# The last slot of a mixture-of-experts stage is activated and rounded in pairs of column blocks, with its remainders and its sum on VectorE

## The chip, the cores and the metric

One core of a Trainium2 chip runs the whole program. The metric is the device time of one execution in microseconds (us); shown is the median of three. The engines are PE (TensorE: matmuls, with its weight loads as PEld), DVE (VectorE), ACT (ScalarE), POOL (GpSimd) and SP (SyncE, which here only issues transfers). A name with q behind it (ACTq, POOLq) is the sequencer of that engine.

## The reference

Three residual blocks on x of 64 x 32 tokens with 256 features; the change touches the last one.

```python
x = x + xattn(layernorm(x), ctx_768)          # 16 heads over 257 context rows
x = x + local_attention(layernorm(x))         # window of 5 tokens
# third block: 8 experts, each token goes to one
logits = t @ Wr + br;  e = argmax(logits)     # t = layernorm(x), 2048 tokens
h = gelu(t @ W1[e] + b1[e])                   # 256 -> 1024
h = gelu(h @ W2[e] + b2[e])                   # 1024 -> 512
x = x + h @ W3[e] + b3[e]                     # 512 -> 256
```

## The kernel before, in words

**Slots.** Once every token has its expert, the tokens are grouped by expert into slots of 128 rows; there are always SLOTS = (2048 + 8 * 127) // 128 = 23 of them, numbered 0 to 22. A slot's rows are fetched from a buffer in DRAM by an indirect transfer (`gather_slot`, L671), which brings the residual row and the normalised row, and the result is written to the output by another (`scatter_slot`, L701); both are issued by POOL. `bounds_check=N_TOKENS - 1` is the highest row that such a transfer may touch, given as a number. `slot_x` and `y` have AHEAD = 5 buffers. Slots 0 to 19 run partly in loops, and 20, 21 and 22 are written out with constant numbers.

**Precision.** Each matrix is kept as a rounded part (HI) and the remainder (LO), and a product is the sum of three: HI x HI, HI x LO, LO x HI (`PRODUCTS`, the activations' part first). So every activation is rounded by ACT into its HI tile, and POOL subtracts that from the exact value into the LO tile.

**One slot through the engines.** PE turns the 256 normalised features (`turn_x`, L1479), multiplies by W1 in two halves (`layer1`, L1488), and turns the result `z1` into eight blocks of 128 x 128, four to a half (`turn_z1`, L1520). ACT adds the bias and applies Gelu block by block (`first_layer`: four ACTIVATE at L853, then one rounding copy of the half at L857), POOL takes the remainder of each half (`lo_h1`, L686), and PE multiplies by W2 with 24 matmuls of 512 columns (`layer2`, L1536: 8 HI x HI, 8 HI x LO, 8 LO x HI). ACT copies the result to `z2` (`copy_z2`, L844), PE turns it (`turn_z2`, four transposes, L1544), ACT applies the second Gelu (`second_layer`: four ACTIVATE at L863, one rounding at L867), POOL takes the remainder (`lo_h2`, L690), and PE multiplies by W3 (`layer3`: one matmul for the bias row at L1551, then 12 of 256 columns at L1556, the last four with the LO part). The product lands in the one bank `ps_y`; ACT copies it to `y` (`copy_y`, L840), which also frees the bank for the next slot (`y_copied`), POOL adds the residual rows (`add_residual`, L696) and issues the scatter.

**Order around the end.** The order of every engine is written out by hand. For slots 21 and 22 it is:

- PE: layer2(21), turn_z1(22), turn_z2(21), layer2(22), layer3(21), turn_z2(22), layer3(22). The third layer of slot 21 is kept back (`postponed`) so that PE has work while ACT copies z2 of slot 22.
- ACT: copy_z2(21), first_layer(22), second_layer(21), copy_z2(22), copy_y(21), second_layer(22), copy_y(22).
- POOL: lo_h1(22), lo_h2(21), add_residual(21), scatter_slot(21), lo_h2(22), add_residual(22), scatter_slot(22).
- DVE splits the experts' weights into HI and LO (L1202, L1205) and has nothing after that.
- SP waits at L514 until all scatters have landed. Every engine then ends with a DRAIN (L52), the end of the block.

`keep_clock(n)` (L1276) issues n transposes of the identity into a bank that is not in use, and computes nothing. It stands before the change in the drain of the attention stages and, with n = 34, ahead of slot 0.

Of the kernel before, what the change touches and what calls it, by code (L numbers as in the profile page):

```python
# [12 lines left out]
ALU = mybir.AluOpType  # L13
AX = mybir.AxisListType

P = 128
# [4 lines left out]
def perceiver_kernel(nc, x, ctx_turned, last_turned, mask, Wq, Wk, Wv, Wo, lWq_turned, lbq, lWk_turned, lbk, lWv, lbv,  # L21
# [30 lines left out]
    with ExitStack() as stack:  # L52
# [10 lines left out]
        def sem(name):  # L63
            return stack.enter_context(nc.semaphore(name))
# [196 lines left out]
        y_filled = sem("y_filled")  # L261
        y_copied = sem("y_copied")
        y_done = sem("y_done")
        y_stored = [sem(f"y_stored{i}") for i in range(AHEAD)]
        w_in = sem("w_in")
        wq_in = sem("wq_in")
# [114 lines left out]
        def turned_rows(i):  # L381

            return (xT_parts_1, xT_raw_1) if isinstance(i, int) and i == 1 else (xT_parts, xT_raw)

        def last_but_one(i):
            return follows(i, 1) and not follows(i, 2)
# [130 lines left out]
        def _(pool):  # L517
# [145 lines left out]

            over_tiles(pool, iteration)

            def gather_slot(i):
                q = i % AHEAD
                if i >= AHEAD:
                    pool.wait_ge(y_done, i - AHEAD + 1)
                    pool.wait_ge(y_stored[q], 16 * (i // AHEAD))  # L670
                g.indirect_dma_start(out=slot_x[:, q, :], out_offset=None, in_=rows_dram,  # L671
                                     in_offset=bass.IndirectOffsetOnAxis(ap=slot_ids[:, i, 0:1], axis=0),
                                     bounds_check=N_TOKENS - 1, oob_is_err=False).then_inc(slot_in[q], 16)

            def lo_xT(i):
                pool.wait_ge(xT_hi_done, i + 1)
# [5 lines left out]
            def lo_h1(i):  # L682
                for half in range(2):
                    fs = slice(half * F1 // P // 2, (half + 1) * F1 // P // 2)
                    pool.wait_ge(h1_hi_done, 2 * i + half + 1)
                    g.tensor_tensor(h1_parts[LO][:, fs, :], h1[:, fs, :], h1_parts[HI][:, fs, :].bitcast(F32), ALU.subtract).then_inc(h1_done, 1)  # L686

            def lo_h2(i):
# [8 lines left out]

            def scatter_slot(i):
                q = i % AHEAD
                pool.wait_ge(y_done, i + 1)  # L700
                g.indirect_dma_start(out=out_rows, out_offset=bass.IndirectOffsetOnAxis(ap=slot_ids[:, i, 1:2], axis=0),  # L701
                                     in_=y[:, q, :], in_offset=None, bounds_check=N_TOKENS - 1, oob_is_err=False).then_inc(y_stored[q], 16)

            pool.wait_ge(rows_done, 16 * TILES)
            pool.wait_ge(route, MAPPED)
            gather_slot(0)
# [7 lines left out]
            for i in range(SLOTS):  # L714
                if i > 0:
                    add_residual(i - 1)
                if i + 3 < SLOTS:
                    gather_slot(i + 3)
                if i > 0:
                    scatter_slot(i - 1)  # L720
                if i + 2 < SLOTS:
                    lo_xT(i + 2)
                if not last_but_one(i):
                    lo_h2(i)
                if i + 1 < SLOTS:
                    lo_h1(i + 1)
                if last_but_one(i):
                    lo_h2(i)
            add_residual(SLOTS - 1)
            scatter_slot(SLOTS - 1)  # L730

        @block.scalar
        def _(act):
# [112 lines left out]
            def first_layer(i, e):  # L846

                for half in range(2):
# [7 lines left out]
                    act.wait_ge(gelu1_done, 2 * i + half + 1)  # L856
                    a.copy(h1_parts[HI][:, 4 * half:4 * half + 4, :], h1[:, 4 * half:4 * half + 4, :]).then_inc(h1_hi_done, 1)  # L857

            def second_layer(i, e):
                act.wait_ge(t2_filled, i + 1)  # L860
                alone(act)
                for c in range(F2 // P):
                    last = a.activation(h2[:, c, :], ps_t2[:, c * P:(c + 1) * P], ACT.Gelu,  # L863
                                        bias=bias_cols[:, bass.ds(e * (F2 // P) + E * F1 // P + c, 1)])
                last.then_inc(gelu2_done, 1)
                act.wait_ge(gelu2_done, i + 1)
                a.copy(h2_parts[HI], h2).then_inc(h2_hi_done, 1)  # L867
# [22 lines left out]

            def slot(i, run, q):
                copy_z2(i)
                if not follows(i, 1):
                    copy_y(i - 1, q - 1)
                if follows(i, 2):
                    copy_xT(i + 2)
                if not last_but_one(i):
                    second_layer(i, expert_of(i))
                if follows(i, 1):
                    first_layer(i + 1, expert_of(i + 1))  # L900
                if last_but_one(i):
                    second_layer(i, expert_of(i))
                if follows(i, 2):
                    copy_z1(i + 2)
                if not last_but_one(i):
                    copy_y(i, q)

            over_slots(act, slot)

# [1 line left out]
        def _(dve):  # L911
# [275 lines left out]
            for first_matrix, e in EARLY + LATE:  # L1187
                w, raw, buffers, w_in_buffer, ready = ((w1, w1_raw, BUFFERS1, w1_in, w1_ready) if first_matrix else
                                                      (w23, w23_raw, BUFFERS23, w23_in, w23_ready))
                b = e % buffers  # L1190
                pieces = [(w_in_buffer[b], slice(0, COLS1))] if first_matrix else zip(w_in_buffer[b], PIECES)
                for n, (piece_in, columns) in enumerate(pieces):
                    dve.wait_ge(piece_in, 16 * (e // buffers + 1))
                    if not first_matrix and e == 1 and n == 0:
                        dve.wait_ge(b3_split, 1)
                    early = (e, None if first_matrix else n) in ROUNDED_EARLY
                    if early:
                        dve.wait_ge(early_rounded, ROUNDED_EARLY.index((e, None if first_matrix else n)) + 1)
                    for at in range(columns.start, columns.stop, 512):
                        part = slice(at, at + 512)  # L1200
                        if not early:
                            d.tensor_copy(w[:, b, HI, part], raw[:, b, part]).then_inc(rounded, 1)  # L1202
                            k += 1
                            dve.wait_ge(rounded, k)
                        last = d.tensor_tensor(w[:, b, LO, part], raw[:, b, part], f32(w[:, b, HI, part]), ALU.subtract)  # L1205
                        if at + 512 == columns.stop:
                            last.then_inc(ready, 1)
                        elif early:
                            last.then_inc(rounded, 1)
                            k += 1  # L1210
                            dve.wait_ge(rounded, k)

        @block.tensor
        def _(pe):
# [312 lines left out]
            def layer2(i, e):  # L1527
                pe.wait_ge(z2_copied, i)
                for products in (PRODUCTS[0:2], PRODUCTS[2:3]):
                    for half in range(2):  # L1530
                        pe.wait_ge(w23_ready, 3 * e + half + 1)
                        for hp, wp in products:
                            for f in range(4 * half, 4 * half + 4):
                                if wp == HI and f == 4 * half:
                                    pe.wait_ge(h1_done if hp == LO else h1_hi_done, 2 * i + half + 1)
                                last = t.matmul(ps_z2[:, :], h1_parts[hp][:, f, :], weight(w23, e % BUFFERS23, wp, f * F2, F2),  # L1536
                                                start=(hp == HI and wp == HI and f == 0), stop=(hp == LO and f == F1 // P - 1))
                last.then_inc(z2_filled, 1)
# [5 lines left out]
                    last = t.transpose(ps_t2[:, c * P:(c + 1) * P], z2[:, c * P:(c + 1) * P], ident[:, :])  # L1544
                last.then_inc(t2_filled, 1)

            def layer3(i, e):
# [4 lines left out]
                for hp, wp in PRODUCTS:  # L1552
                    if hp == LO:
                        pe.wait_ge(h2_done, i + 1)
                    for c in range(F2 // P):
                        last = t.matmul(ps_y[:, 0:D], h2_parts[hp][:, c, :], weight(w23, e % BUFFERS23, wp, W3_AT + c * D, D),  # L1556
                                        start=False, stop=(hp == LO and c == F2 // P - 1))
                last.then_inc(y_filled, 1)

            def expert_of(i):  # L1560
# [11 lines left out]
            def slot(i, run, q):  # L1572
                expert = expert_of(i)
                layer2(i, expert)
                if postponed:
                    layer3(i - 1, postponed.pop())
                if follows(i, 2):
                    ahead = expert_of(i + 2)
                    turn_x(i + 2, run + (q + 2) // AHEAD, (q + 2) % AHEAD)
# [47 lines left out]
```

## Time and profile before

| what | value |
|---|---|
| median of 3 executions | 760.08 us |
| lowest, highest | 759.63, 761.08 us |
| the profiled execution, its own time | 763.91 us |
| span of the instructions in its trace | 762.2 us |
| mean granted TensorE clock in it | 0.972 of 2.4 GHz |
| busy: PE, PEld, DVE, ACT, POOL | 94%, 80%, 62%, 59%, 57% of the span |
| chain of work that ended last | PE 85%, DVE 7%, ACT 2%, POOL 1% of the span |

The profiled execution took 763.91 us, of which 762.2 us lie between its first and its last instruction; it is 3.83 us above the median of the unprofiled ones. Times inside the trace count from the first instruction. A granted clock of 1.00 is 2.4 GHz and 0.50 is 1.2 GHz.

### The profile page before, as it was taken

What the parts mean: (1) busy time and instruction counts of PE and PEld (TensorE: products, weight loads), DVE (VectorE), ACT (ScalarE), POOL (GpSimd) and SP (SyncE); (2) the same over time, 40 slices, a digit from 0 to 9 for tenths busy, and PEclk for the clock granted to TensorE, in tenths of its full rate; (3) what the DMA queues carried; (4) which work ended last, traced back from release to release, by engine and by line L of the source; (5) the groups of instructions that cost most, each with busy time, mean ns of one, the idle gap of its engine ahead of it and who ended that gap; (6) DMA issues with size and microseconds to landing.
All of it is one profiled execution on the core that took longest, in us unless ns stands there. A gap on an engine that the chain in (4) does not pass through costs nothing.

```text
span 762.2 us, 26478 instructions
## 1 busy us (share of the span) xinstructions
PE 717.5 (94%) x9229; PEld 609.4 (80%) x9230; DVE 472.0 (62%) x1377; ACT 452.8 (59%) x1072; POOL 431.3 (57%) x565
## 2 busy tenths in 40 slices
PE   8999999999999999999999648999999999997994
PEld 7788888888888888888888547888788888886873
DVE  4556677767776776777767559979824871196000
ACT  4646666666666666666665044566575756654762
POOL 6456656565656565656553504576767666574643
PEclk9989999999999999999999888999999999998997
DMA  7222232323233323333226403246026412360000
GB/s 220 85 71 80 71 97 76 90 76 90 76 90 77 88 76 90 81 85 75 86 71 253 170 15 98 91 165 227 25 95 228 157 37 77 134 214 17 21 7 1
DMA packets 55012, 73.93 MB, mean 97 GB/s; under 512 B 5839, under 2 KB 40688, under 8 KB 54962
## 3 DMA queue, kind: packets, MB, share of 16 engines
q1 hardware_dynamic: 48820, 60.35, 26.8%
q0 software_dynamic: 2944, 8.13, 3.5%
q10 hardware_dynamic: 3200, 4.80, 1.7%
q8 instruction: 30, 0.49, 0.3%
q14 instruction: 18, 0.15, 0.1%
HBM read 66.91 MB, written 7.27 MB: 97 GB/s over the span
## 4 chain that ended last, share of the span: by engine, by line
PE 85%; DVE 7%; ACT 2%; issue 2%; DMA 2%; POOL 1%; SPq 0%; POOLq 0%; ACTq 0%; DVEq 0%
PE ps_s L1536 16%; PE ps_kv L1231 10%; PE ps_kv L1223 10%; PE ps_p L1270 7%; PE ps_s L1242 5%; PE ps_o L1256 5%; PE ps_o L1556 4%; PE ps_p L1488 4%; PE ps_kv L1488 4%; PE ps_m L1367 2%; DVE w L1205 2%; PE ps_m L1301 2%; PE ps_m L1324 2%; PE ps_s L1520 2%; PE ps_m L1372 2%
## 5 line engine op out<-in xcount | busy, mean ns | idle before, releaser
L746 ACT ACTIVATE prob<-prob,neg_max 128x257 f32<-128x257 f32 x256 | 111.2, 500 | 46.1 <-DVE neg_max L939 44.5
L939 DVE CUSTOM_DVE_ANT_0 prob<-ps_s,mask_add 128x257 f32<-128x257 f32 x256 | 94.8, 422 | 66.0 <-PE ps_s L1242 66.0
L1202 DVE CAST w<-w_raw 128x512 fp32r<-128x512 f32 x94 | 67.2, 715 | 71.7 <-DMA w_raw<-in_L_ffn_W_dram 71.7
L1205 DVE TENSOR_TENSOR w<-w_raw,w 128x512 fp32r<-128x512 f32 x112 | 101.1, 906 | 3.7
L1536 PE MATMUL ps_s<-w,h_hi 128*128 x368 | 93.8, 407 | 9.1 <-DVE w L1205 3.9
L585 POOL TENSOR_TENSOR ctx_parts<-ctx_raw,ctx_parts 128x512 fp32r<-128x512 f32 x64 | 82.7, 1292 | 32.4 <-ACT ctx_parts L741 31.6
L1536 PEld LDWEIGHTS ps_s<-w,h_hi 128*128 128x128 f32 x368 | 68.8, 191 | 28.0 <-issue 13.2
L1223 PE MATMUL ps_kv<-ctx_parts,wkv_hi 128*128 128x256 f32 x512 | 86.7, 297 | 0.2 <-POOL ctx_parts L585 0.2
L1231 PE MATMUL ps_kv<-wkv_hi,ctx_parts 128*128 128x256 f32 x512 | 84.9, 294 | 1.0 <-ACT kT L750 0.7
L1270 PE MATMUL ps_p<-ident,prob 128*128 128x128 f32 x512 | 77.9, 274 | 0.9 <-DVE probT L961 0.8
L686 POOL TENSOR_TENSOR h_lo<-h,h_hi 128x512 fp32r<-128x512 f32 x46 | 62.0, 1348 | 26.2 <-ACT h_hi L857 25.9
L754 ACT COPY v<-ps_kv 128x512 f32<-128x512 f32 x64 | 37.5, 585 | 65.8 <-PE ps_kv L1231 65.8
L1223 PEld LDWEIGHTS ps_kv<-ctx_parts,wkv_hi 128*128 128x128 f32 x512 | 71.8, 193 | 2.3 <-issue 0.4
L1231 PEld LDWEIGHTS ps_kv<-wkv_hi,ctx_parts 128*128 128x128 f32 x512 | 69.3, 189 | 3.5 <-ACT kT L750 2.0
L578 POOL TENSOR_TENSOR ctx_raw<-ctx_raw,last_ctxT 128x512 f32<-128x512 f32 x64 | 69.4, 1084 | 1.3 <-DMA ctx_raw<-in_ctx_turned_dram 1.3
L961 DVE COPY probT<-ps_p 128x512 f32<-128x512 f32 x64 | 44.1, 689 | 35.8 <-PE ps_p L1270 34.3
L844 ACT COPY lqk<-ps_s 128x512 f32<-128x512 f32 x23 | 13.5, 586 | 88.1 <-PE ps_s L1536 88.1
L598 POOL COPY last_prob<-prob 128x4 f32<-128x4 f32 x64 | 12.0, 187 | 91.2 <-ACT prob L746 88.1
L1270 PEld LDWEIGHTS ps_p<-ident,prob 128*128 128x128 f32 x512 | 60.6, 141 | 3.5 <-DVE probT L961 1.0
L853 ACT ACTIVATE h<-ps_s,bias_cols 128x128 f32<-128x128 f32 x184 | 52.3, 367 | 4.9 <-issue 3.9
L750 ACT COPY kT<-ps_kv 128x512 f32<-128x512 f32 x64 | 37.2, 582 | 27.6 <-PE ps_kv L1223 27.5
L1256 PEld LDWEIGHTS ps_o<-v,probT 128*32 128x32 f32 x4096 | 41.3, 110 | 14.1 <-issue 13.8
(201 smaller groups left out, 1558.6 us busy)
## 6 DMA issues: line engine op xcount, KB each, us to landing
w_raw<-in_L_ffn_W_dram SPq DMA_DIRECT2D x24, 1024.0 KB, 6.9
ctx_raw<-in_ctx_turned_dram SPq DMA_DIRECT2D x63, 256.0 KB, 3.4
mask_add<-mask_dram SPq DMA_DIRECT2D x64, 128.5 KB, 3.4
rows_dram<-x3n ACTq DMA_DIRECT2D x16, 256.0 KB, 4.3
w_raw<-in_L_ffn_W_dram SPq DMA_DIRECT2D x8, 512.0 KB, 4.1
xt<-in_x_dram SPq DMA_DIRECT2D x16, 128.0 KB, 2.1
xr<-in_x_dram SPq DMA_DIRECT2D x16, 128.0 KB, 2.2
slot_x<-rows_dram,slot_ids POOLq DMA_INDIRECT x23, 3.7
```

The lines of the kernel that those rows point to most:

```text
L578: g.tensor_tensor(ctx_raw[:, b, :, :], ctx_raw[:, b, :, :], last_ctxT[:, :, bass.ds(n, 1)].to_broadcast([P, 2, JM]), ALU.subtract).then_in ...
L585: g.tensor_tensor(ctx_parts[:, b % 2, 2:4, :], ctx_raw[:, b, :, :], ctx_parts[:, b % 2, 0:2, :].bitcast(F32), ALU.subtract).then_inc(split ...
L686: g.tensor_tensor(h1_parts[LO][:, fs, :], h1[:, fs, :], h1_parts[HI][:, fs, :].bitcast(F32), ALU.subtract).then_inc(h1_done, 1)
L746: a.activation(prob[:, g, :], prob[:, g, :], ACT.Exp, bias=neg_max[:, g:g + 1], scale=-1.0).then_inc(exp_done, 1)
L939: d.tensor_tensor_reduce(prob[:, r, :], ps_s[r][:, 0:J], mask_add[:, k, :], -(HD ** -0.5), 3.0e38, ALU.add, ALU.min, neg_max[:, r:r + 1]). ...
L1202: d.tensor_copy(w[:, b, HI, part], raw[:, b, part]).then_inc(rounded, 1)
L1205: last = d.tensor_tensor(w[:, b, LO, part], raw[:, b, part], f32(w[:, b, HI, part]), ALU.subtract)
L1223: last = t.matmul(ps_kv[:, half * JM:(half + 1) * JM], w[:, 0, r, half * P:(half + 1) * P], ctx_parts[:, buffer, c, :], start=(i == 0), st ...
L1231: last = t.matmul(ps_kv[:, jt * D:(jt + 1) * D], ctx_parts[:, buffer, c, jt * P:(jt + 1) * P], w[:, 1, r, :], start=(i == 0), stop=(i == 4))
L1256: last = t.matmul(ps_o[h * S:(h + 1) * S, g * BLOCK:(g + 1) * BLOCK], probT[:, jt, g * P + h * S:g * P + (h + 1) * S], v[:, k % 2, jt, g / ...
L1270: last = t.transpose(ps_p[:, g * P:(g + 1) * P], prob[:, g, jt * P:(jt + 1) * P], ident[:, :])
L1536: last = t.matmul(ps_z2[:, :], h1_parts[hp][:, f, :], weight(w23, e % BUFFERS23, wp, f * F2, F2), start=(hp == HI and wp == HI and f == 0) ...
```

## The change

For slot 22 alone (`LAST`):

1. ACT's `first_layer_last` and `second_layer_last` handle two blocks at a time: two ACTIVATE, then a rounding copy of 256 columns, four times for the first layer and twice for the second. `layer2` waits for the HI part pair by pair, and `lo_h1` on POOL after every second pair.
2. In slot 22 PE runs layer2(22), the HI part of layer3(21) (`layer3_hi`, bias and 8 matmuls), turn_z2(22), the LO part of layer3(21) (`layer3_lo`, 4 matmuls), then `keep_clock(11)`, then `layer3_last`, which waits for `y_copied`, then for the HI pairs and the LO pairs.
3. ACT runs copy_z2(22), second_layer_last, copy_y(21). There is no copy_y(22).
4. DVE takes the remainders of the second layer of slot 22 in two pairs, and adds `ps_y` and the residual rows straight into `y` (`last_y_done`). POOL has no lo_h2(22) and no add_residual(22); its last scatter waits for `last_y_done`.
5. For all slots, `bounds_check` of the 46 indirect transfers is a register `last_row`, set once by `reg_mov`.

```diff
+            last_row = pool.alloc_register("last_row")
             def gather_slot(i):
...
-                                     bounds_check=N_TOKENS - 1, oob_is_err=False).then_inc(slot_in[q], 16)
+                                     bounds_check=last_row, oob_is_err=False).then_inc(slot_in[q], 16)
...
-                    pool.wait_ge(h1_hi_done, 2 * i + half + 1)
+                    pool.wait_ge(h1_hi_done, 2 * i + (2 if i == LAST else 1) * (half + 1))
...
             def scatter_slot(i):
-                pool.wait_ge(y_done, i + 1)
+                if i == LAST:
+                    pool.wait_ge(last_y_done, 1)
+                else:
+                    pool.wait_ge(y_done, i + 1)
...
+            pool.reg_mov(last_row, N_TOKENS - 1)
...
-                if not last_but_one(i):
+                if not last_but_one(i) and i != LAST:
                     lo_h2(i)
...
-            add_residual(SLOTS - 1)
-            scatter_slot(SLOTS - 1)
+            scatter_slot(LAST)
...
+            def first_layer_last(e):
+                for pair in range(4):
+                    act.wait_ge(t1_filled, 2 * LAST + pair // 2 + 1)
+                    alone(act)
+                    for c in range(2):
+                        f = 2 * pair + c
+                        last = a.activation(h1[:, f, :], ps_t1[pair // 2][:, f % 4 * P:(f % 4 + 1) * P], ACT.Gelu,
+                                            bias=bias_cols[:, bass.ds(e * (F1 // P) + f, 1)])
+                    last.then_inc(gelu1_done, 1)
+                    act.wait_ge(gelu1_done, 2 * LAST + pair + 1)
+                    a.copy(h1_parts[HI][:, 2 * pair:2 * pair + 2, :], h1[:, 2 * pair:2 * pair + 2, :]).then_inc(h1_hi_done, 1)
+
+            def second_layer_last(e):
+                act.wait_ge(t2_filled, SLOTS)
+                act.wait_ge(h2_done, LAST)
+                for pair in range(2):
+                    alone(act)
+                    for c in range(2 * pair, 2 * pair + 2):
+                        last = a.activation(h2[:, c, :], ps_t2[:, c * P:(c + 1) * P], ACT.Gelu,
+                                            bias=bias_cols[:, bass.ds(e * (F2 // P) + E * F1 // P + c, 1)])
+                    last.then_inc(gelu2_done, 1)
+                    act.wait_ge(gelu2_done, LAST + pair + 1)
+                    a.copy(h2_parts[HI][:, 2 * pair:2 * pair + 2, :], h2[:, 2 * pair:2 * pair + 2, :]).then_inc(h2_hi_done, 1)
...
+                if is_last(i):
+                    second_layer_last(expert_of(i))
                     copy_y(i - 1, q - 1)
+                    return
...
+            dve.wait_ge(y_filled, LAST)
+            for pair in range(2):
+                dve.wait_ge(h2_hi_done, LAST + pair + 1)
+                d.tensor_tensor(h2_parts[LO][:, 2 * pair:2 * pair + 2, :], h2[:, 2 * pair:2 * pair + 2, :],
+                                f32(h2_parts[HI][:, 2 * pair:2 * pair + 2, :]), ALU.subtract).then_inc(h2_done, 1)
+            dve.wait_ge(y_filled, SLOTS)
+            dve.wait_ge(slot_in[LAST % AHEAD], 16 * (LAST // AHEAD + 1))
+            d.tensor_tensor(y[:, LAST % AHEAD, :], ps_y[:, 0:D], slot_x[:, LAST % AHEAD, 0:D], ALU.add).then_inc(last_y_done, 1)
...
+                                elif wp == HI and is_last(i) and f % 2 == 0:
+                                    pe.wait_ge(h1_hi_done, 2 * i + f // 2 + 1)
...
+            def layer3_last(e):
+                pe.wait_ge(y_copied, LAST)
+                t.matmul(ps_y[:, 0:D], ones_r[:, :], b3_parts[:, bass.ds(e * D, D)], start=True, stop=False)
+                for pair in range(2):
+                    pe.wait_ge(h2_hi_done, LAST + pair + 1)
+                    layer3_products(e, PRODUCTS[0:2], range(2 * pair, 2 * pair + 2))
+                for pair in range(2):
+                    pe.wait_ge(h2_done, LAST + pair + 1)
+                    last = layer3_products(e, PRODUCTS[2:3], range(2 * pair, 2 * pair + 2))
                 last.then_inc(y_filled, 1)
...
-                if postponed:
-                    layer3(i - 1, postponed.pop())
+                if is_last(i):
+                    other = postponed.pop()
+                    layer3_hi(i - 1, other)
+                    turn_z2(i)
+                    layer3_lo(i - 1, other)
+                    keep_clock(11)
+                    layer3_last(expert)
+                    return
```

## Rows read from the trace of the kernel before

**Rows 1.** The chain that ended last: start us, length us, what.
```profile
728.20 0.44 PE ps_s L1544 x4
...
741.84 5.86 PE ps_s L1536 x24
747.70 0.12 PE ps_o L1551
747.82 1.43 PE ps_o L1556 x12
...
749.36 0.30 ACT y L840
...
752.26 0.38 PE ps_o L1551
752.64 2.33 PE ps_o L1556 x12
...
755.09 0.38 ACT y L840
...
755.61 0.73 POOL y L696
...
756.36 0.03 POOLq L701
...
756.90 1.21 POOLq L52
```

**Rows 2.** The timeline of slots 21 and 22: start us, length us, engine, line.
```profile
739.75 1.14 ACT L853 ACTIVATE h<-ps_s,bias_cols 128x128 f32<-128x128 f32 x4
740.93 0.62 ACT L857 CAST h_hi<-h 128x512 fp32r<-128x512 f32 x1
741.45 1.13 ACT L853 ACTIVATE h<-ps_s,bias_cols 128x128 f32<-128x128 f32 x4
...
750.12 1.14 ACT L863 ACTIVATE x3n<-ps_s,bias_cols 128x128 f32<-128x128 f32 x4 [0.39 <-PE ps_s L1544]
751.29 0.62 ACT L867 CAST h_hi<-x3n 128x512 fp32r<-128x512 f32 x1
751.39 0.98 POOL L701 DMA_INDIRECT out_dram<-y,slot_ids  x1 [0.80 <-POOL y L696]
...
752.39 1.30 POOL L690 TENSOR_TENSOR h_lo<-x3n,h_hi 128x512 fp32r<-128x512 f32 x1
...
757.12 0.99 POOL L701 DMA_INDIRECT out_dram<-y,slot_ids  x1 [0.80 <-POOL y L696]
```

**Rows 3.** POOL's closing instruction: ns (min/median/max), first and last start us.
```profile
L52 POOLq DRAIN  x1: 5053/5053/5053, 756.9 to 756.9; - x1
```

**Rows 4.** Stretches: us, PE, PEld, DVE, ACT, POOL busy, PEclk, DMA, GB/s.
```profile
461.00:462.00 1.00, 1.00 (x6) 1.00 (x5) 0.88 (x4) 0.00 (x0) 0.00 (x0) 0.50 0.00 0
...
464.00:465.00 1.00, 1.00 (x12) 1.00 (x11) 0.96 (x2) 0.00 (x0) 0.65 (x1) 1.00 0.83 233
...
754.00:755.00 1.00, 0.96 (x4) 0.67 (x4) 0.00 (x0) 0.00 (x0) 0.00 (x0) 0.50 0.00 0
```

**Rows 5.** The timeline of an ordinary slot: from transposes to Gelu.
```profile
492.93 0.60 PE L1544 MATMUL ps_s<-ident,lqk 128*128 128x128 f32 x4
...
493.76 1.14 ACT L863 ACTIVATE x3n<-ps_s,bias_cols 128x128 f32<-128x128 f32 x4 [0.58 <-PE ps_s L1544]
```

**Rows 6.** The timeline ahead of slot 0: transposes that compute nothing.
```profile
460.06 5.52 PE L1276 MATMUL ps_s<-ident 128*128 128x128 f32 x34
```

**Rows 7.** Groups by line and shape on DVE: count, busy us, mean ns, idle.
```profile
L1007 DVE TENSOR_TENSOR x<-ps_m,xr 128x256 f32<-128x256 f32 x16 | 6.7, 421 | 2.2 <-PE ps_m L1367 2.2
...
L1045 DVE TENSOR_TENSOR wkv_lo<-wkv,wkv_hi 128x256 fp32r<-128x256 f32 x2 | 1.7, 849 | 3.4 <-ACT wkv_hi L797 1.8 <-ACT wkv_hi L793 1.6
```

**Rows 8.** POOL's timeline: a scatter issued right behind a gather.
```profile
714.02 1.02 POOL L701 DMA_INDIRECT out_dram<-y,slot_ids  x1 [0.31 <-issue]
```

**Rows 9.** The 23 scatters (L701): time from issue to landing.
```profile
DMA to landing us min/median/max: 2.1/2.7/6.0
```

More of the change, by code:

```diff
@@ L263, in perceiver_kernel @@
         y_done = sem("y_done")
+        last_y_done = sem("last_y_done")
         y_stored = [sem(f"y_stored{i}") for i in range(AHEAD)]
@@ L383, in turned_rows, with is_last @@
             return (xT_parts_1, xT_raw_1) if isinstance(i, int) and i == 1 else (xT_parts, xT_raw)
+        LAST = SLOTS - 1
+        def is_last(i):
+            return isinstance(i, int) and i == LAST
         def last_but_one(i):
@@ L699, in scatter_slot @@
                 q = i % AHEAD
-                pool.wait_ge(y_done, i + 1)
+                if i == LAST:
+                    pool.wait_ge(last_y_done, 1)
+                else:
+                    pool.wait_ge(y_done, i + 1)
                 g.indirect_dma_start(out=out_rows, out_offset=bass.IndirectOffsetOnAxis(ap=slot_ids[:, i, 1:2], axis=0),
-                                     in_=y[:, q, :], in_offset=None, bounds_check=N_TOKENS - 1, oob_is_err=False).then_inc(y_stored[q], 16)
+                                     in_=y[:, q, :], in_offset=None, bounds_check=last_row, oob_is_err=False).then_inc(y_stored[q], 16)
+            pool.reg_mov(last_row, N_TOKENS - 1)
             pool.wait_ge(rows_done, 16 * TILES)
@@ L892, in slot @@
                 copy_z2(i)
-                if not follows(i, 1):
+                if is_last(i):
+                    second_layer_last(expert_of(i))
                     copy_y(i - 1, q - 1)
+                    return
                 if follows(i, 2):
                     copy_xT(i + 2)
-                if not last_but_one(i):
+                if last_but_one(i):
+                    first_layer_last(expert_of(i + 1))
                     second_layer(i, expert_of(i))
[L899 to L902, printed above, removed]
+                    return
+                second_layer(i, expert_of(i))
+                first_layer(i + 1, expert_of(i + 1))
                 if follows(i, 2):
                     copy_z1(i + 2)
-                if not last_but_one(i):
-                    copy_y(i, q)
+                copy_y(i, q)
             over_slots(act, slot)
@@ L1533, in layer2 @@
                             for f in range(4 * half, 4 * half + 4):
-                                if wp == HI and f == 4 * half:
-                                    pe.wait_ge(h1_done if hp == LO else h1_hi_done, 2 * i + half + 1)
+                                if hp == LO and f == 4 * half:
+                                    pe.wait_ge(h1_done, 2 * i + half + 1)
+                                elif wp == HI and is_last(i) and f % 2 == 0:
+                                    pe.wait_ge(h1_hi_done, 2 * i + f // 2 + 1)
+                                elif wp == HI and not is_last(i) and f == 4 * half:
+                                    pe.wait_ge(h1_hi_done, 2 * i + half + 1)
                                 last = t.matmul(ps_z2[:, :], h1_parts[hp][:, f, :], weight(w23, e % BUFFERS23, wp, f * F2, F2),
@@ L1545, in turn_z2, with layer3_products, layer3_hi @@
                 last.then_inc(t2_filled, 1)
-            def layer3(i, e):
+            def layer3_products(e, products, chunks):
+                for hp, wp in products:
+                    for c in chunks:
+                        last = t.matmul(ps_y[:, 0:D], h2_parts[hp][:, c, :], weight(w23, e % BUFFERS23, wp, W3_AT + c * D, D),
+                                        start=False, stop=(hp == LO and c == F2 // P - 1))
+                return last
+            def layer3_hi(i, e):
                 pe.wait_ge(w23_ready, 3 * e + 3)
@@ L1551, in layer3, with layer3_lo @@
                 t.matmul(ps_y[:, 0:D], ones_r[:, :], b3_parts[:, bass.ds(e * D, D)], start=True, stop=False)
[L1552 to L1557, printed above, removed]
+                layer3_products(e, PRODUCTS[0:2], range(F2 // P))
+            def layer3_lo(i, e):
+                pe.wait_ge(h2_done, i + 1)
+                layer3_products(e, PRODUCTS[2:3], range(F2 // P)).then_inc(y_filled, 1)
+            def layer3(i, e):
+                layer3_hi(i, e)
+                layer3_lo(i, e)
+            def layer3_last(e):
[7 more added lines that the diff above has]
+                    last = layer3_products(e, PRODUCTS[2:3], range(2 * pair, 2 * pair + 2))
                 last.then_inc(y_filled, 1)
@@ L1574, in slot @@
                 layer2(i, expert)
-                if postponed:
-                    layer3(i - 1, postponed.pop())
+                if is_last(i):
[5 more added lines that the diff above has]
+                    layer3_last(expert)
+                    return
                 if follows(i, 2):
```

## The prediction

> **What bounds the kernel now.** I read the chain of work that ended last first, and of it only the end, since five of the six edits touch slot 22 alone. PE holds 85% of the chain over the whole run, but behind the last big product it does not: from 747.70 us on the chain goes from engine to engine [rows 1]. Next I read the timeline of the same stretch, to see what each engine did besides [rows 2]; then the closing instruction [rows 3]; then the granted clock [rows 4].
>
> The end reads so. ACT starts the first layer of slot 22 at 739.75, rounds the first half from 740.93 to 741.55 [rows 2], and 0.29 later, at 741.84, PE starts layer2(22), whose 24 matmuls end at 747.70 [rows 1]. layer3(21) takes until 749.25 and the copy of its result until 749.66 [rows 1]. Only then does ACT start the second Gelu, at 750.12, and its rounding ends at 751.91 [rows 2]. PE starts layer3(22) at 752.26 and ends at 754.97 [rows 1]. ACT copies, POOL adds until 756.34, the scatter starts at 757.12, and POOL's closing DRAIN, begun at 756.90, runs 5.05 us to 761.95 [rows 1 to 3]. So from 747.70 on everything is latency: a microsecond that the last scatter starts earlier should be one off the end, as long as the DRAIN keeps its length behind it.
>
> **The change part by part, each as the new time of an event.**
>
> *First layer in pairs.* Four Gelu blocks take 1.14 and a rounding of 512 columns 0.62; the second half starts 1.70 after the first, 0.06 less than the two durations together [rows 2]. A pair I put at 0.62 for two blocks (half of 1.14, and a little for the one that overlaps nothing) and 0.38 for 256 columns, the time of ACT's copy of y [rows 1]; with the gap of 0.04 between and the overlap with the next pair, one pair every 0.94 (estimate). The first rounding then ends at 740.79 and PE starts at 741.08, 0.76 early. It does not keep that: after two matmuls of 0.244 (5.86 / 24, [rows 1]) it is at 741.57 and waits for pair 1 (741.73 + 0.29 = 742.02). Later pairs are in time (pair 3 is there at 743.90, wanted at 743.97). 22 matmuls of 0.244 from 742.02 end at 747.39, against 747.70: **-0.31**. The four pairs end 0.36 later than the two halves, which delays the rounding of slot 21's second layer to about 745.7; it is wanted at 747.4. That cover of 1.7 hides it.
>
> *Turning z2 before the LO part.* The bias matmul and 8 products take 0.12 + 8 x 0.119 = 1.07, so they end at 748.46; the four transposes take 0.44 [rows 1]: 748.90. In an ordinary slot Gelu starts 0.23 after them (493.76 against 492.93 + 0.60, [rows 5]), which gives 749.13 against 750.12, since ACT no longer copies y first: **-0.68** more.
>
> *Second layer in pairs, the copy behind it.* Pair 0 is rounded at 750.17, pair 1 at 751.11. But `layer3_last` first waits for `y_copied`, and copy_y(21) now stands behind both pairs on ACT. With 0.38 and a little overlap it ends at 751.45. So the pairs cannot let PE start early; PE starts with both there. The gate moves from 751.91 to 751.45, so this step gives **0.53 back**. Behind the copy wait POOL's add and scatter of slot 21: 751.45 + 0.14 + 0.73 + 0.78 puts that scatter at 753.1 instead of 751.39 and its end at 754.1.
>
> *The last product.* PE starts 0.35 after its gate (752.26 - 751.91), at 751.80. Before, it took 0.38 + 2.33 = 2.71. The same 12 matmuls took 1.43 for slot 21 [rows 1], so I take 0.38 + 1.43 = 1.81 and an end at 753.61: **-0.90**. Two things were in the way. POOL's remainder ran from 752.39 to 753.69 behind the scatter of slot 21 [rows 2], but PE wanted it at about 753.59, so that is 0.1. The other 0.8 is the clock, at 0.50 between 754 and 755 [rows 4], after PE had stood idle from 749.7 to 752.26. Now the 11 transposes fill this: the LO part ends at 749.39, 11 x 0.11 takes PE to 750.60, and 1.2 us stay idle. Their cover is the 0.85 to the gate; even at the 0.16 a piece of 5.52 / 34 [rows 6] they end at 751.2. DVE's remainders of 256 columns are bounded by 0.42 (an add from PSUM of that width) and 0.85 (a subtraction of that shape, [rows 7]); the second ends at 752.1 at the latest, wanted at 753.1. Nothing follows on DVE, whose weights are long done.
>
> Do such transposes hold the clock? The 34 ahead of slot 0 start at 460.06 with the clock at 0.50, and at 464 it is 1.00 [rows 4, 6], with nothing else of weight on PE. The Trainium skill's page "TensorE: Matmul & The Clock Gate", section "Part 4: PE-mode transpose", says that transposes do not count as activity for the clock and full clock does not engage for them. This trace disagrees with it. By the page the 11 would be for nothing and the time would be that of the first rival below.
>
> *DVE's sum.* From PE's end to the end of POOL's add were 756.34 - 754.97 = 1.37. Now about 0.10 of wake-up and 0.42 for an add from PSUM (L1007, [rows 7]): 754.13. **-0.85**.
>
> *The last scatter.* It started 0.78 after the sum (757.12 - 756.34). Now the sum comes from another engine; I keep 0.78: 754.91. The floor is the scatter of slot 21, which ends at 754.1, and a scatter issued right behind another transfer follows in 0.31 [rows 8]: 754.4. So slot 21's scatter is half a microsecond from being the gate, and isn't. Sum so far 757.12 - 754.91 = **-2.21**.
>
> *The register.* Each of the 46 transfers has a MOVE of 0.03 on POOL's sequencer [rows 1]. It lies on the path before the last scatter and before the first gather: **-0.06** with the gaps around it unchanged. Elsewhere POOL waits for others. The bounds are 0 and 46 x 0.03 = 1.4, if every one were on the path. I take the low end.
>
> In sum -2.3: the profiled execution would go from 763.91 to 761.6 (span 762.2 to 759.9), and the median of 760.08 to **757.8**.
>
> **The rivals.**
>
> *The clock gives nothing.* Either the 11 transposes don't hold it, or it did not fall in the timed executions of the kernel before, of which only one is traced. The 0.8 stays: 758.6. For it: the profile of one execution can't speak for the others. Against it: [rows 4, 6], and 2.6 us of idle PE is the longest stretch in the last slots. Chance 0.15.
>
> *Pairs and waits cost more.* Each pair adds a semaphore round trip; 0.35, as PE's wake-up behind ACT, instead of 0.04 would add 0.3 for each of the two pairs that gate PE in the first layer and the two of the second: 1.2, so 759.0. Also here: a scatter that waits for DVE starting later than 0.78. The 0.04 between Gelu and rounding speaks against it. Chance 0.13.
>
> *The end does not follow.* If the DRAIN's end hangs not on the last scatter but on when POOL last had two transfers under way, or on a fixed time, the gain is swallowed and the time is 760.0 (no change). For it: its 5.05 us are more than the 2.1 of the quickest landing [rows 9], so something else than landing sets it. Chance 0.08.
>
> *Slower: the last two scatters collide.* They started 5.7 us apart and will start 1.8 apart. If the last one lands as the slowest did, after 6.0 instead of 2.1 [rows 9], and the DRAIN waits out the landing, 3.9 come on top of -2.3: 761.7. It decides from 2.3 more, a landing after 4.4. Against it: 128 rows of 1 KB are little, and no other traffic is left. Chance 0.04.
>
> *The register is worth more.* If POOL gates slots more than the chain shows, up to 1.4 more: 756.4. Chance 0.07.
>
> **How the numbers follow.** The forecast has 0.53 and a range of its own of 757.2 to 758.4 (0.2 each for the pair's length, the wake-ups and the scatter). The rivals above hold 0.47 together. Leaving out the case of no change, the slower one and half of the register's leaves 0.8 in **756.7 to 759.2**. 0.2% is 1.5 us, about what a measurement of this kernel tells from no change. Below 758.56 lie the forecast, the register's case and about half of the first two (where only part of their price is paid): 0.73. Within: the other halves and the end that does not follow, 0.22. Slower: 0.05.
>
> **What would show it.** In the profile of the changed kernel: layer2(22) starts 0.7 early and stops once for 0.4; the second Gelu starts 0.23 behind the transposes; ACT's copy of y stands behind two roundings and PE starts 0.35 behind it, with all pairs there; PEclk is 1.00 to the end of L1556; the last scatter starts 0.8 behind DVE's sum and at least 0.31 behind slot 21's; the DRAIN is still 5.0 long. The prediction is wrong if the clock was not lost in timed runs, if the last scatter waits longer for DVE or for its predecessor, or if the DRAIN grows by what comes before it shrinks.

## The result, and the profile after

| | before | changed |
|---|---|---|
| median of 15 executions | 761.08 us | 758.05 us |
| lowest, highest | 758.09, 762.59 | 754.54, 759.62 |
| profiled: span | 762.2 | 757.5 |
| mean granted clock in the profile | 0.972 | 0.978 |

The ratio is 0.9958, 95% interval 0.9946 to 0.9971: 3.2 us faster (2.2 to 4.1), worked out on 761.08. The forecast was 757.8, 2.3 us below the 760.08 known then. So the direction held and the gain is somewhat larger than forecast. That the 757.8 lies within 0.3 of the measured 758.05 is partly luck: the median of the kernel before rose by 1.00 with more executions, and the gain was put 0.7 too low.

The two profiled executions differ by 4.64 us, more than the medians do. To split that, I count a **tail**: from the first matmul of layer2(21) to the start of the last scatter. In the chain of the kernel before it starts at 733.14:

```profile
733.14 5.87 PE ps_s L1536 x24
```

[rows 2] have the scatter at 757.12, so this tail is 23.98. The same two events after the change, in the chain and the timeline:

```profile
731.41 5.86 PE ps_s L1587 x24
```
```profile
752.48 0.98 POOL L712 DMA_INDIRECT out_dram<-y,slot_ids  x1 [0.68 <-DVE y L1258]
```

The tail is 21.07, **2.91 shorter**. The other 1.73 lie ahead of anything that the change moves. They are mostly due to TensorE's clock. The same stretch of both kernels by windows, before and then after (columns as in [rows 4]):

```profile
40.00:50.00 10.00, 10.00 (x138) 8.30 (x138) 4.43 (x18) 4.26 (x9) 5.13 (x18) 0.66 0.30 92
```
```profile
40.00:50.00 10.00, 10.00 (x193) 8.45 (x194) 5.57 (x25) 4.92 (x11) 5.26 (x19) 0.83 0.30 94
```

A mean clock of 0.66 means 6.8 us at half clock and one of 0.83 means 3.4. Those 3.4 us more at half clock are worth up to 1.7 us, since PE is busy all the time in both windows (an estimate from these two rows). The attention code that runs here is the same. So the tail, which agrees with the medians, is what the change is judged by.

The changed tail as the timeline shows it (start, length, engine, line; it answers to [rows 2]):

```profile
738.02 0.63 ACT L877 ACTIVATE h<-ps_s,bias_cols 128x128 f32<-128x128 f32 x2
738.67 0.41 ACT L881 CAST h_hi<-h 128x256 fp32r<-128x256 f32 x1
738.99 0.62 ACT L877 ACTIVATE h<-ps_s,bias_cols 128x128 f32<-128x128 f32 x2
...
739.37 4.39 PE L1587 MATMUL ps_s<-w,h_hi 128*128 x16 [0.78 <-ACT h_hi L881]
...
746.53 0.60 PE L1595 MATMUL ps_s<-ident,lqk 128*128 128x128 f32 x4
...
746.88 0.72 PE L1601 MATMUL ps_o<-w,h_lo 128*128 x4
...
747.38 0.62 ACT L890 ACTIVATE x3n<-ps_s,bias_cols 128x128 f32<-128x128 f32 x2 [1.13 <-PE ps_s L1595]
747.44 1.36 PE L1323 MATMUL ps_s<-ident 128*128 128x128 f32 x11
...
749.00 0.40 ACT L894 CAST h_hi<-x3n 128x256 fp32r<-128x256 f32 x1
749.31 0.36 ACT L851 COPY y<-ps_o 128x256 f32<-128x256 f32 x1
749.43 0.43 DVE L1254 TENSOR_TENSOR h_lo<-x3n,h_hi 128x256 fp32r<-128x256 f32 x1 [0.46 <-ACT h_hi L894]
...
749.81 0.38 PE L1623 MATMUL ps_o<-b_parts,ones_r 128*128 x1 [1.00 <-ACT y L851]
749.81 0.73 POOL L704 TENSOR_TENSOR y<-y,slot_x 128x256 f32<-128x256 f32 x1 [4.06 <-ACT y L851]
...
750.82 0.98 POOL L712 DMA_INDIRECT out_dram<-y,slot_ids  x1 [0.28 <-POOL y L704]
...
751.11 0.63 PE L1601 MATMUL ps_o<-w,h_lo 128*128 x4
751.78 0.42 DVE L1258 TENSOR_TENSOR y<-ps_o,slot_x 128x256 f32<-128x256 f32 x1 [1.92 <-PE ps_o L1601]
```

The weight loads (PEld) that belong to its last four matmuls:

```profile
750.99 0.54 PEld L1601 LDWEIGHTS ps_o<-w,h_lo 128*128 128x128 f32 x4
```

Read it from its end. PE ends at 751.74, DVE's sum at 752.20, the scatter starts at 752.48. PE started at 749.81 because of ACT's copy of slot 21's result (the bracket names L851), not because of the rounding at L894, which had ended at 749.40. And both scatters stand 0.28 behind the sum ahead of them; in [rows 2] the number in that place is 0.80. The closing DRAIN is as long as in [rows 3]:

```profile
L52 POOLq DRAIN  x1: 5058/5058/5058, 752.2 to 752.2; - x1
```

By event, each counted from the start of layer2(21):

| event | before | after | gain so far | forecast |
|---|---|---|---|---|
| layer2(22) starts | 8.70 | 7.96 | 0.74 | 0.76 |
| layer2(22) ends | 14.56 | 14.22 | 0.34 | 0.31 |
| second Gelu starts | 16.98 | 15.97 | 1.01 | 0.99 |
| gate of the last product | 18.77 | 18.26 | 0.51 | 0.46 |
| PE ends | 21.83 | 20.33 | 1.50 | 1.36 |
| sum ends | 23.20 | 20.79 | 2.41 | 2.21 |
| last scatter starts | 23.98 | 21.07 | 2.91 | 2.24 |

The gate is what PE waits for: the rounding of the second layer before (it ends at 751.91), ACT's copy of slot 21's result after (749.67). Every row but the last is within 0.2 of its forecast. The last is off by 0.67, of which 0.5 arise between the sum and the scatter.

### The profile page after: what moved, and what is told of

Its sections match the earlier page's. It is cut to its first block, busy times and chain, and to the rows that moved or that the text cites. A ratio compares the mean times of both kernels' runs of the same rounds, so it can differ in the third digit from the quotient of the medians.

```text
span 757.5 us, 26459 instructions
## 1 busy us (share of the span) xinstructions
PE 717.2 (95%) x9240; PEld 610.1 (81%) x9241; DVE 474.5 (63%) x1380; ACT 452.7 (60%) x1074; POOL 427.5 (56%) x563
## 4 chain that ended last, share of the span: by engine, by line
PE 86%; DVE 7%; ACT 2%; issue 2%; DMA 1%; POOL 1%; POOLq 0%; ACTq 0%; DVEq 0%
PE ps_s L1587 16%; PE ps_kv L1278 11%; PE ps_kv L1270 10%; PE ps_p L1317 7%; PE ps_o L1303 5%; PE ps_s L1289 5%; PE ps_kv L1535 4%; PE ps_p L1535 4%; PE ps_o L1601 4%; PE ps_m L1414 2%; DVE w L1243 2%; PE ps_m L1348 2%; PE ps_s L1567 2%; PE ps_m L1371 2%; PE ps_m L1419 2%
## 5 line engine op out<-in xcount | busy, mean ns | idle before, releaser
L1243 DVE TENSOR_TENSOR w<-w_raw,w 128x512 fp32r<-128x512 f32 x112 | 103.4, 926 | 3.7
L864 ACT ACTIVATE h<-ps_s,bias_cols 128x128 f32<-128x128 f32 x176 | 50.1, 367 | 4.8 <-issue 3.9
```

## The experiments

All are judged by their tails, since a half-clock stretch upstream moves single times by more than the effects: layer2(21) started between 727.05 and 731.75 in these twelve profiles. Each tail comes from one execution. How well it repeats can be seen from kernels that ran more than once with the clock at 1.00 through their tail: 21.07 twice (the changed kernel, and e2, which is in effect the same), and 21.14 and 21.17 (e4 and e11).

### The row limit

**e1.** The changed kernel, with the number again, for gathers and scatters alike:

```diff
-                                     bounds_check=last_row, oob_is_err=False)
+                                     bounds_check=N_TOKENS - 1, oob_is_err=False)
```

> The changed kernel with the row limit as a number again in all 46 transfers; all else kept. The tail is counted from the first matmul of layer2(21) to the start of the last scatter: 23.98 us before the change, 21.07 after it. Theory (the limit's MOVE stands between the wait and the transfer and holds the transfer back by 0.5): the gap from the end of POOL's or DVE's sum to the scatter goes from 0.28 back to 0.80, the tail to 21.6, while scatters issued right behind a gather keep their 0.31. Rival (the MOVE costs its own 0.03 only, as predicted, and the shorter gap has another cause, such as DVE's sum): the gap stays at 0.28 to 0.31, the tail at 21.1.

Measured: tail 21.60. The last scatter started at 752.75, 0.80 behind DVE's sum (751.53 + 0.42), and that of slot 21 also 0.80 behind its own. The chain shows where the time goes:

```profile
749.58 0.74 POOL y L704
750.32 0.03 issue
750.35 0.03 POOLq L712
750.38 0.73 issue
751.11 0.92 POOL out_dram L712
```

The chain shown is that of slot 21's scatter. The MOVE takes 0.03 and starts 0.03 behind the sum, and then 0.73 pass before the transfer starts; with the register 0.28 pass in all. The register is worth 0.53 on the path.

**e2.** A MOVE to another register between wait and scatter. The edit gives one to every scatter, the last too, unlike what was written ahead of it:

```diff
+            other = pool.alloc_register("other")
...
                     pool.wait_ge(y_done, i + 1)
+                pool.reg_mov(other, 1)
                 g.indirect_dma_start(out=out_rows, ...
```

> The changed kernel with the limit in its register, and one MOVE to a register that nothing reads, between the wait and each scatter of slots 0 to 21 (the last scatter has none). Theory (any instruction that takes the wait leaves the transfer to be prepared behind it): the gap behind POOL's sum is 0.80 for the scatters of slots 19 to 21, as before the change, and the last one keeps 0.28. Rival (the transfer waits for the register that it reads to be written): the gap stays 0.28 for all.

Measured: tail 21.07, all gaps 0.28. It settles nothing: the trace holds no MOVE on that line. Nothing reads the register; in e1, where nothing reads `last_row` any more, the trace has no MOVE on the line that sets it either. e9 asks the question again, with registers that are read.

**e3.** The kernel before with the register alone (every line of the change with `last_row` in it, for gathers and scatters).

> The kernel before with the register alone, all else as before. Theory: gaps of 0.28 instead of 0.80 behind POOL's sum; the remainder of slot 22 on POOL, which stood behind the scatter of slot 21, starts 0.5 earlier too; the tail goes from 23.98 to 23.4. Rival (the MOVE costs its 0.03): tail 23.9.

Measured: all gaps 0.28, but a tail of 23.91. In this execution the clock fell earlier, ahead of the last product and not in it. The product by windows and in the timeline:

```profile
750.00:751.00 1.00, 0.36 (x1) 0.37 (x2) 0.00 (x0) 0.28 (x1) 0.86 (x2) 0.73 0.03 1
751.00:752.00 1.00, 1.00 (x6) 1.00 (x6) 0.00 (x0) 0.00 (x0) 0.63 (x1) 0.50 0.06 16
```
```profile
750.64 0.58 PE L1554 MATMUL ps_o<-b_parts,ones_r 128*128 x1 [2.60 <-ACT h_hi L870]
...
751.01 1.91 PE L1559 MATMUL ps_o<-w,h_hi 128*128 x8
...
752.72 1.05 PE L1559 MATMUL ps_o<-w,h_lo 128*128 x4
```

It took 3.13 from 750.64 to 753.77, against 2.71 in [rows 1]. The 0.42 lost there hides most of the 0.5 won behind it. So the tail of this run decides between neither of the two expectations; the gaps do.

**e9.** Where does the MOVE have to stand to cost this? The scatter of slot 19 reads a register written before its wait, that of slot 20 one written behind it; behind slot 21's wait stands a MOVE that its scatter does not read.

```diff
+                limit = {LAST - 3: before_wait, LAST - 2: after_wait, LAST: unread}.get(i, last_row)
+                if i == LAST - 3:
+                    pool.reg_mov(before_wait, N_TOKENS - 1)
...
                     pool.wait_ge(y_done, i + 1)
+                if i == LAST - 2:
+                    pool.reg_mov(after_wait, N_TOKENS - 1)
+                if i == LAST - 1:
+                    pool.reg_mov(unread, N_TOKENS - 1)
```

> e2 turned out to hold no MOVE at all: nothing read the register, and its trace has no such instruction. So here the changed kernel with three live MOVEs: the scatter of slot 19 reads a register written just before its wait; that of slot 20 reads one written between wait and scatter; between the wait of slot 21 and its scatter a register is written that only the scatter of slot 22 reads. Gap from the end of POOL's sum to the scatter. Theory A (whatever instruction stands first behind the wait takes the wait, and the transfer is prepared only behind it): 0.28, 0.80, 0.80. Theory B (a transfer can't be prepared until the register that it reads is written): 0.28, 0.80, 0.28. Tail with A and B 21.1 or up to 21.3 (slot 21's scatter 0.5 later, close to being the gate).

Measured, the four scatters in order:

```profile
719.52 1.02 POOL L719 DMA_INDIRECT out_dram<-y,slot_ids  x1 [0.28 <-POOL y L704]
...
732.02 0.99 POOL L719 DMA_INDIRECT out_dram<-y,slot_ids  x1 [0.80 <-POOL y L704]
...
747.96 0.98 POOL L719 DMA_INDIRECT out_dram<-y,slot_ids  x1 [0.80 <-POOL y L704]
749.24 0.98 POOL L719 DMA_INDIRECT out_dram<-y,slot_ids  x1 [0.30 <-issue]
```

0.28, 0.80, 0.80: theory A. A MOVE between the wait and the transfer delays the transfer by 0.5, whether or not the transfer reads its register; ahead of the wait it costs nothing that shows (0.28). That the transfer is prepared while the wait lasts, if nothing stands between, is the reading that fits; the trace has no record of the preparation itself. The tail is 21.24: with slot 21's scatter half a microsecond later, it became the gate of the last one, which starts 0.30 behind it, as the scatter in [rows 8] starts 0.31 behind a gather.

### The clock

**e4, e11, e12.** Three executions of the changed kernel without the transposes:

```diff
-                    keep_clock(11)
```

> The changed kernel without the 11 transposes ahead of layer3_last. PE is then idle for about 2.2 us between the LO part of layer3(21) and layer3_last, instead of 1.0. Theory (the transposes hold the clock): the granted clock falls to 0.50 in or around layer3_last in this execution or in some, the 13 matmuls take up to 3.1 instead of 1.93, the tail up to 22.2. It may not fall in a single execution, since the idle time is 0.4 shorter than in the kernel before. Rival (transposes don't count, the shorter idle time and the order of the work saved the clock): 1.00 to the end, tail 21.1.

> e4 again, whose clock held with PE idle for 2.2 us. Theory (without transposes it depends on the execution whether the clock falls): 1.00 and a tail of 21.1, or a fall and a tail of 21.5 to 22.2. If neither this nor the next falls, the shorter idle time was enough by itself here.

> The same kernel as e4 and e11 a third time, with the same expectation as e11: 1.00 and a tail of 21.1, or a fall and 21.5 to 22.2.

Measured: tails 21.14, 21.17 and 22.16. In e4 and e11 the clock held through 2.2 us of idle PE; in e12 it fell in the product:

```profile
747.00:748.00 1.00, 1.00 (x5) 0.90 (x6) 0.02 (x1) 0.00 (x0) 0.72 (x2) 0.79 0.03 8
748.00:749.00 1.00, 1.00 (x7) 1.00 (x6) 0.00 (x0) 0.00 (x0) 0.96 (x1) 0.50 0.07 16
```
```profile
747.26 1.84 PE L1601 MATMUL ps_o<-w,h_hi 128*128 x8
748.90 1.05 PE L1601 MATMUL ps_o<-w,h_lo 128*128 x4
```

So the transposes buy 1.1 us in an execution that would have caught a fall and 0.07 to 0.10 in one that would not. That the clock fell in one of three is all that the runs say of how often.

**e10.** The kernel before with transposes alone:

```diff
                 turn_z2(i)
+                if not follows(i, 1):
+                    keep_clock(20)
```

> The kernel before with 20 transposes of the identity between turn_z2(22) and layer3(22), where PE was idle for 2.6 us, and nothing else. Theory (they hold the clock; the wait for the remainder on POOL stays): 1.00 to the end of the last product, which takes about 1.9 to 2.1 instead of 2.71, tail 23.3. Rival (transposes don't count as activity): the clock falls as in the kernel before and in e3, the tail stays at 24.0 or more.

Measured: tail 23.55, and a clock of 1.00 through the product. Where PE had been idle for 2.6 us it now stood for 0.25. The product took 2.38 (749.15 to 751.53):

```profile
749.36 1.26 PE L1556 MATMUL ps_o<-w,h_hi 128*128 x8
749.44 1.29 POOL L690 TENSOR_TENSOR h_lo<-x3n,h_hi 128x512 fp32r<-128x512 f32 x1
750.78 0.53 PEld L1556 LDWEIGHTS ps_o<-w,h_lo 128*128 128x128 f32 x4 [0.37 <-POOL h_lo L690]
750.79 0.74 PE L1556 MATMUL ps_o<-w,h_lo 128*128 x4 [0.17 <-POOL h_lo L690]
```

The weight loads of the LO part (PEld) stand for 0.37 until POOL's remainder is there. Against the 1.93 of the changed kernel this waiting costs 0.45. It is longer than it was in the kernel before, since POOL's remainder ends 1.58 behind PE's start here (750.73 against 749.15) and 1.43 there (753.69 against 752.26). So the time before the change can't be split by taking 2.38 from 2.71. What can be compared is the stretch from the end of the remainder to the end of the product: 0.80 here, at full clock, and 1.28 there. The window and the rows of the kernel before:

```profile
753.00:754.00 1.00, 1.00 (x7) 0.76 (x6) 0.00 (x0) 0.00 (x0) 0.69 (x1) 0.76 0.02 0
```
```profile
753.74 0.93 PEld L1556 LDWEIGHTS ps_o<-w,h_lo 128*128 128x128 f32 x4 [0.24 <-POOL h_lo L690]
753.74 1.22 PE L1556 MATMUL ps_o<-w,h_lo 128*128 x4
```

A mean of 0.76 in this window and 0.50 in the next ([rows 4]) puts the fall at about 753.5, so it is the LO part that ran at half clock. The clock cost 0.48 there, and the wait for the remainder about 0.30, the rest of the 0.78 between 2.71 and 1.93.

### The other parts

**e5.** The second layer in one piece (four ACTIVATE, one rounding of 512 columns; DVE's two remainders behind it).

```diff
-                for pair in range(2):
-                    alone(act)
-                    for c in range(2 * pair, 2 * pair + 2):
+                alone(act)
+                for c in range(F2 // P):
...
-                    a.copy(h2_parts[HI][:, 2 * pair:2 * pair + 2, :], h2[:, 2 * pair:2 * pair + 2, :]).then_inc(h2_hi_done, 1)
+                a.copy(h2_parts[HI], h2).then_inc(h2_hi_done, 1)
```

> The changed kernel with the second layer of slot 22 activated as four blocks and rounded once on ACT; DVE still takes two remainders, both after that one rounding. Theory (PE waits for the copy of slot 21 behind both pairs, so pairs only cost ACT time): the copy of y ends 0.26 earlier, PE starts layer3_last 0.26 earlier, tail 20.8. Rival (pairs let part of the product or the remainders start earlier): tail 21.1 or more.

Measured: tail 20.85. The pairs of the second layer lose 0.22: PE waits for slot 21's copy behind both, so the extra ACT time delays it and nothing starts earlier.

**e6.** The first layer in two halves again (`first_layer`, and the waits as before).

```diff
-                    first_layer_last(expert_of(i + 1))
+                    first_layer(i + 1, expert_of(i + 1))
```

> The changed kernel with the first layer of slot 22 in two halves again. Theory: layer2(22) starts 0.7 later and runs without a stop, so it ends 0.3 later; tail 21.4. Rival (the early start was worth its whole 0.7): tail 21.8.

Measured: tail 21.40. The pairs of the first layer win 0.33, not the 0.74 by which layer2 starts early.

**e7.** The last sum as before: ACT's copy and POOL's add in place of DVE's sum.

```diff
                     copy_y(i - 1, q - 1)
+                    copy_y(i, q)
...
-            d.tensor_tensor(y[:, LAST % AHEAD, :], ps_y[:, 0:D], slot_x[:, LAST % AHEAD, 0:D], ALU.add).then_inc(last_y_done, 1)
...
+            add_residual(LAST)
             scatter_slot(LAST)
```

> The changed kernel with the last sum as before: ACT copies ps_y to y, POOL adds the residual rows, DVE only takes remainders. Theory: 1.37 from PE's end to the sum's end instead of 0.46, tail 22.0. Rival (the last scatter was held by the scatter of slot 21 on POOL anyway, so DVE's sum is worth less): tail 21.3 to 21.7.

Measured: tail 22.01. DVE's sum is worth 0.94. That DVE takes the remainders too, in place of POOL, was not undone by a run of its own.

**e8.** A version that takes away the gate which e5 points at: another bank for the last product, and slot 21's sum on DVE too.

```diff
-                if i == LAST:
-                    pool.wait_ge(last_y_done, 1)
+                if i >= LAST - 1:
+                    pool.wait_ge(last_y_done, i - LAST + 2)
...
-                if i > 0:
+                if 0 < i < LAST:
                     add_residual(i - 1)
...
                     second_layer_last(expert_of(i))
-                    copy_y(i - 1, q - 1)
...
             dve.wait_ge(y_filled, LAST)
+            dve.wait_ge(slot_in[(LAST - 1) % AHEAD], 16 * ((LAST - 1) // AHEAD + 1))
+            d.tensor_tensor(y[:, (LAST - 1) % AHEAD, :], ps_y[:, 0:D], slot_x[:, (LAST - 1) % AHEAD, 0:D], ALU.add).then_inc(last_y_done, 1)
...
-                pe.wait_ge(y_copied, LAST)
-                t.matmul(ps_y[:, 0:D], ones_r[:, :], b3_parts[:, bass.ds(e * D, D)], start=True, stop=False)
+                t.matmul(ps_p[:, 0:D], ones_r[:, :], b3_parts[:, bass.ds(e * D, D)], start=True, stop=False)
...
-                    keep_clock(11)
+                    keep_clock(8)
```

The products of `layer3_last` and DVE's last sum use `ps_p` as well.

> A version meant to beat both: slot 22's third layer accumulates in the bank ps_p, free by then, so it waits for no copy; DVE adds the residual of slot 21 too (no copy_y(21) on ACT, no add_residual(21) on POOL), and 8 transposes stand instead of 11. Theory (the copy of slot 21 behind the pairs is the gate of layer3_last): PE starts with pair 0, ends pair 1 and both remainders about 1.0 earlier, the last scatter starts 1.0 earlier, tail 20.1; against the kernel before 4 us or 0.5% faster. Rival (the remainders or POOL's scatter of slot 21 gate next): tail 20.6 to 21.1.

Measured: tail 20.20, 0.87 less than the changed kernel. Its median is 756.85 us of 6 executions, beside 761.59 of the kernel before on the same chip; the ratio is 0.9945, interval 0.9923 to 0.9966. That interval overlaps the changed kernel's, so the timing shows it faster than the kernel before, and only the tail of one execution sets it apart from the changed one. The gate is now the rounding of the second pair:

```profile
746.53 0.75 PE L1602 MATMUL ps_p<-w,h_hi 128*128 x4
746.95 0.40 ACT L894 CAST h_hi<-x3n 128x256 fp32r<-128x256 f32 x1
...
747.50 0.83 PE L1602 MATMUL ps_p<-w,h_hi 128*128 x4 [0.21 <-ACT h_hi L894]
```

## Why the prediction was right, point by point

*First layer in pairs*, -0.31: the profile has -0.34 and undoing it costs 0.33. As forecast, PE starts early, stops once, and ends a third of a microsecond early.

*Turning z2 before the LO part*, -0.68: the two profiles give -0.67 between the end of layer2(22) and the second Gelu, which starts 0.25 behind the transposes. No run undid it alone.

*Second layer in pairs, the copy behind it*, +0.53: +0.50. e5 shows that the pairs themselves are 0.22 of this, and the rest is the copy of y, which stands there in e5 too.

*The last product*, -0.90: -0.99. The sum held by luck, since its terms did not. I put 0.1 on the wait for POOL's remainder and 0.8 on the clock; they were 0.30 and 0.48 (e10, and the rows shown there). The step that failed is "PE wanted it at about 753.59": it is the weight loads that wait, ahead of the matmuls. In the changed kernel, where nothing holds them, those of the LO part start 1.18 behind PE (750.99 against 749.81). In the kernel before that would have been 753.44, and they started at 753.74, 0.30 late. The other 0.2 comes from PE starting 0.14 behind its gate where I had 0.35. What the clock costs is not one number: 0.48 in the trace that I had, 1.0 in e12 against e4 and e11, and 1.20 in e3, whose product took 3.13 with its remainder in time.

*DVE's sum*, -0.85: -0.91 in the two profiles, 0.94 when undone.

*The last scatter and the register*. Here the size was off. "The register, -0.06" was priced by the length of the MOVE; on the path before the last scatter it measured 0.53 (e1). The row was in front of me: a gap of 0.80 behind POOL's sum in [rows 2], with the MOVE in it in [rows 1]. I took the 0.78 for the cost of a wait and not for that of the MOVE's place. My upper bound, 46 MOVEs of 0.03, multiplied the wrong thing: it is 0.5 for each of the scatters whose wait lasts. Ahead of the tail it adds nothing that shows: from the first gather to layer2(21) pass 271.11 us before (462.03 to 733.14) and 271.04 after (460.37 to 731.41), and a scatter that follows a gather at once does so in 0.31 before and 0.30 after. At the first gather the gap behind DVE's `slot_ids` shrank only from 1.05 to 0.97; why not by 0.5 stays open.

*Rivals.* "The clock gives nothing" had two conditions. That transposes don't hold the clock fell: in all nine traces with transposes ahead of the last product it stayed at 1.00 to the product's end, and in three of the five without them it did not (before, e3, e12). This speaks against what the prediction tells from the Trainium skill's page "TensorE: Matmul & The Clock Gate", section "Part 4: PE-mode transpose". How often the clock fell in the timed executions of the kernel before is not shown. "Pairs and waits cost more" fell by the table and by the gap of 0.28 in place of 0.78. "The end does not follow" and the collision of the last scatters fell with the DRAIN, 5.05 to 5.06 long in both, and with the span ending 5.05 behind the start of the last scatter in every one of the twelve experiments, also with the two scatters 1.3 us apart (e9).

Put together: 2.24 forecast for the tail, 0.5 more for the register and 0.2 over the other steps (2.41 against 2.21 at the end of the sum) give 2.9.

## What to carry to other kernels

When a wait ends a chain, look at what the first instruction behind it is: here a MOVE of 0.03 between a wait and an indirect transfer cost 0.5, so set registers ahead of the wait. Splitting a step in pairs wins only as far as the next wait of the consumer reaches; find that wait first (here the copy of another slot's result out of a shared bank; in e8, taking that gate away together with ACT's copy and POOL's add was worth 0.87). And measure a change at the end of a long program by a tail between two events of the trace, since what happens upstream moves the whole time by more.

## What the runs showed of the hardware that I had not expected

- An indirect transfer started 0.28 us behind the event it waits for, and 0.80 when a MOVE stood between (e1, e9).
- Executions of one kernel differ in their half-clock stretches: in e4, e11 and e12, the same kernel, layer2(21) started at 730.79, 729.23 and 728.53, and only the third lost its clock in the last product.
- Of two DVE remainders back to back in e5 the first took 0.43 and the second 0.98, where they take 0.42 to 0.43 each in the changed kernel. POOL's add ran beside the second; whether that or something else is the cause was not tested. PE was not delayed:

```profile
L1253 DVE TENSOR_TENSOR h_lo<-x3n,h_hi x2: 426/704/983, 746.6 to 747.0; 128x256 fp32r<-128x256 f32 x2
```
```profile
746.62 1.33 DVE L1253 TENSOR_TENSOR h_lo<-x3n,h_hi 128x256 fp32r<-128x256 f32 x2 [49.77 <-ACT h_hi L893]
...
746.93 0.73 POOL L704 TENSOR_TENSOR y<-y,slot_x 128x256 f32<-128x256 f32 x1 [3.83 <-ACT y L851]
```
